# Two attention layers and two mixture-of-experts layers on one core: the small PSUM bank visited once per slot, the values product two slots behind, and one fp16 copy moved from ScalarE to VectorE

## What is computed

```python
xn = ln(x, g_norm)
q = (xn @ Wq).reshape(b, n, HEADS, DIM_HEAD).transpose(0, 2, 1, 3)
kv = xn @ Wkv
k, v = (kv[..., :DIM_HEAD], kv[..., DIM_HEAD:])
...
q = l2norm(q) * q_scale
k = l2norm(k) * k_scale
sim = jnp.einsum('bhid,bjd->bhij', q, k) * SCALE
...
sim = jnp.where(causal, neg, sim)
...
attn = jax.nn.softmax(sim, axis=-1)
out = jnp.einsum('bhij,bjd->bhid', attn, v)
out = out.transpose(0, 2, 1, 3).reshape(b, n, HEADS * DIM_HEAD)
return ln(out @ Wout, g_out)
```

## Time and profile before

| | |
|---|---|
| median of three runs | 1735.61 us |
| the profiled execution: its time | 1732.54 us |
| its span, first to last instruction | 1730.6 us |
| attention (first to last `probs`) | 90.0 to 1355.8 us |
| mixture of experts | from about 1370 us on |
| mean granted TensorE clock | 0.972 |

### The profile page before, as it was taken

One profiled execution on the slowest core, in us unless ns is written; L12 is line 12 of the kernel. 1 busy time (PEld: TensorE's weight loads), 2 busy tenths in 40 slices (PEclk: granted clock), 3 DMA queues, 4 the chain that ended last, 5 costly groups with the idle time before them and its releaser, 6 DMA issues.

```text
span 1730.6 us, 46424 instructions
## 1 busy us (share of the span) xinstructions
PE 1470.3 (85%) x16377; PEld 1081.0 (62%) x16377; DVE 1410.4 (81%) x3651; ACT 1210.2 (70%) x3064; POOL 751.0 (43%) x1412
## 2 busy tenths in 40 slices
PE   2467778888889999977888888999999799999998
PEld 1245556666677777766666666777777555555555
DVE  4557778888889999977788888999999687777777
ACT  1268778888889899978888888989999432332232
POOL 5557776443434334366554232223222365522222
PEclk9779999999999999989999999999999899999999
DMA  4002122111211223012121212221223000000000
GB/s 138 7 24 62 51 62 75 57 62 69 75 58 67 87 99 99 33 44 62 51 81 52 85 63 75 75 81 62 82 99 99 1 25 19 1 1 1 13 13 25
DMA packets 50440, 96.70 MB, mean 56 GB/s; under 512 B 3332, under 2 KB 27028, under 8 KB 50212
## 3 DMA queue, kind: packets, MB, share of 16 engines
q1 hardware_dynamic: 45504, 90.27, 15.8%
q10 hardware_dynamic: 4708, 3.45, 0.7%
HBM read 91.54 MB, written 2.17 MB: 54 GB/s over the span
## 4 chain that ended last, share of the span: by engine, by line
PE 42%; DVE 21%; ACT 14%; issue 11%; POOL 3%; DMA 1%; DVEq 0%; ACTq 0%; SPq 0%; POOLq 0%
PE tp L1312 7%; DVE p_lo L964 7%; ACT p_hi L722 6%; DVE biased L880 5%; PE sc L1203 3%; PE sc L1086 3%; PE sc L1087 3%; PE sc L1088 3%; ACT q_b L651 3%; PE sc L1204 3%; ACT probs L630 3%; PE op L1086 2%; PE aux L1086 2%; PE tp L1086 2%; PE aux L1088 2%
## 5 line engine op out<-in xcount | busy, mean ns | idle before, releaser
L964 DVE TENSOR_TENSOR p_lo<-tp,p_hi 128x512 f16<-128x512 f32 (+3 forms) x768 | 416.6, 554 | 121.3 <-ACT p_hi L722 114.3
L880 DVE CUSTOM_DVE_ANT_0 biased<-sc,bias,neg_null 128x256 f32<-128x256 f32 (+7 forms) x512 | 411.0, 803 | 2.7 <-issue 0.8
L630 ACT ACTIVATE probs<-biased,neg_max 128x256 f32<-128x256 f32 (+7 forms) x512 | 395.7, 773 | 14.2 <-DVE neg_max L880 12.7
L1312 PE MATMUL tp<-ident,probs 128*128 128x128 f32 x2304 | 388.7, 278 | 17.7 <-DVE p_lo L964 15.5
L722 ACT ACTIVATE p_hi<-tp 128x512 f16<-128x512 f32 (+3 forms) x768 | 368.9, 491 | 43.6 <-PE tp L1312 33.5
L1086 PE MATMUL op<-v_s,p_hi 128*128 128x64 f16 x2304 | 284.9, 194 | 54.4 <-DVE p_lo L964 35.9
L1203 PE MATMUL sc<-k_a,q_a 128*128 128x512 f16 (+3 forms) x768 | 254.2, 331 | 66.2 <-DVE neg_max L880 59.3
L1312 PEld LDWEIGHTS tp<-ident,probs 128*128 128x128 f32 x2304 | 267.9, 142 | 52.9 <-issue 37.9
L1088 PE MATMUL op<-v_s,p_lo 128*128 128x64 f16 x2304 | 284.0, 194 | 0.0
L1087 PE MATMUL op<-v_s,p_hi 128*128 128x64 f16 x2304 | 283.9, 194 | 0.0
L1086 PEld LDWEIGHTS op<-v_s,p_hi 128*128 128x128 f16 x2304 | 216.0, 99 | 85.5 <-DVE p_lo L964 62.1
(11 more groups left out here) (257 smaller groups left out, 3611.4 us busy)
## 6 DMA issues: line engine op xcount, KB each, us to landing
bias<-rel_table SPq DMA_DIRECT2D x4, 2048.0 KB, 8.5
bias<-in_fside_16xSxS SPq DMA_DIRECT2D x4, 2048.0 KB, 7.9
bias<-rel_table SPq DMA_DIRECT2D x4, 1792.0 KB, 7.9
bias<-in_fside_16xSxS SPq DMA_DIRECT2D x4, 1792.0 KB, 7.1
bias<-rel_table SPq DMA_DIRECT2D x4, 1536.0 KB, 7.3
bias<-in_fside_16xSxS SPq DMA_DIRECT2D x4, 1536.0 KB, 6.7
bias<-rel_table SPq DMA_DIRECT2D x4, 1280.0 KB, 5.6
bias<-in_fside_16xSxS SPq DMA_DIRECT2D x4, 1280.0 KB, 6.3
```

The lines of the kernel that those rows point to most:

```text
L630: ac.activation(probs[:, i % 2, 0:w], biased[:, i % 2, 0:w], ACT.Exp, bias=neg_max[:, u % 2, i % HU:i % HU + 1], scale=-1.0, accum_out=row ...
L880: ve.tensor_tensor_reduce(out=biased[:, i % 2, 0:w], in0=sc[i % 2][:, 0:w], in1=bias[:, g % 2, i % HU, 0:w], scale=-1.0, scalar=neg_null[: ...
L964: ve.tensor_tensor(p_lo[:, gi % 4, 0:nb * P], tp[gi % 2][:, 0:nb * P], p_hi[:, gi % 4, 0:nb * P], ALU.subtract).then_inc(s["p_lo"], 1)
L1312: last = te.transpose(tp[gi % 2][:, jj * P:(jj + 1) * P], probs[:, n % 2, (j0 + jj) * P:(j0 + jj + 1) * P], ident[:, :])
```

## The change

All of it lies in the per-slot order. TensorE: the small jobs come last in the slot, one per slot (k0 `null` and `y`, into different columns of one bank, k1 `q_proj`, k2 `q_t`, k3 `ot`), and the values product is that of slot n-2. Their evictions come at the start of the next slot: on ScalarE ahead of `probs`, on VectorE behind `biased`. `o_raw` and what hangs on it move one slot later, `q_t` one slot earlier. The copy `q_dup` is issued by VectorE, ahead of `q_lo`. The transposes of x move from n0-15 to n0-14. The numbers and sizes of all other instructions stay as they are.

```diff
-            return 0 <= n < N - 4 and all(plan.tile(i) < TILES // 2 for i in range(n + 1, n + 4))
+            return 0 <= n < N - 6 and all(plan.tile(i) < TILES // 2 for i in range(n + 1, n + 6))
...
                 first, second = banks(n)
+                was_first, was_second = banks(n - 1)
+                if k == 1 and 0 <= m - 2 < NU:
+                    u = m - 2
+                    act.wait_ge(s["y"], u + 1)
...
+                    ac.activation(dst, was_first[:, 0:D], ACT.Copy, scale=1.0 / WS).then_inc(s["y_s"], 1)
+                if k == 3 and 0 <= m + 2 < NU:
+                    u = m + 2
+                    act.wait_ge(s["q_t"], u + 1)
...
+                    for e in range(2):
+                        ac.activation(heads(q_b[0:DH, u % 2, :], e),
+                                      was_first[e * DH:(e + 1) * DH, 0:UW].rearrange("p (c q) -> p c q", q=P), ACT.Copy)\
+                            .then_inc(s["q_hi"], 1)
...
-                    act.wait_ge(s["q_hi"], 2 * (u + 1))
-                    ac.activation(q_a[0:DH, u % 2, :], q_b[0:DH, u % 2, :], ACT.Copy).then_inc(s["q_dup"], 1)
...
-                if k == 1 and 1 <= m <= NU:
+                was_first, was_second = banks(n - 1)
+                if k == 2 and 1 <= m <= NU:
                     u = m - 1
                     dve.wait_ge(s["o_null"], u + 1)
-                    dve.wait_ge(s["pv"], plan.groups_done(n - 2))
+                    dve.wait_ge(s["pv"], plan.groups_done(n - 3))
...
                     dve.wait_ge(s["q_hi"], 2 * (u + 1))
+                    ve.tensor_copy(q_a[0:DH, u % 2, :], q_b[0:DH, u % 2, :]).then_inc(s["q_dup"], 1)
...
+                if k == 1 and 0 <= m + 1 < NU:
...
+                    dve.wait_ge(s["q_null"], u + 1)
+                    if 0 <= m - 2 < NU:
+                        dve.wait_ge(s["y_s"], m - 1)
...
+                if k == 0 and 0 <= m - 2 < NU:
+                    u = m - 2
+                    dve.wait_ge(s["ot_hi"], u + 1)
...
+                now, before = plan.at(n), plan.at(n - 2)
...
+                if k == 0 and 0 <= m + 1 < NU:
+                    u = m + 1
+                    layer = u // U0
+                    pe.wait_ge(s["q_dup"], u + 1)
+                    pe.wait_ge(s["q_lo"], 2 * (u + 1))
...
-                if k == 3 and 0 <= m + 2 < NU:
+                if k == 2 and 0 <= m + 2 < NU:
...
-                now, before = plan.at(n), plan.at(n - 1)
...
+                if k == 3 and 0 <= m - 1 < NU:
+                    u = m - 1
+                    take(False, (s["ot_lo"], u + 1))
+                    pe.wait_ge(s["o_n"], u + 1)
```

More of the change, by code:

```diff
@@ L481, in _ @@
                         .then_inc(s["o_n"], 1)
-                if k == 2 and 0 <= m + 3 < U0:
+                if k == 3 and 0 <= m + 3 < U0:
                     u = m + 3
@@ L967, in _ @@
                         small()
-                if k == 1 and 0 <= m + 3 < U0:
+                if k == 2 and 0 <= m + 3 < U0:
                     u = m + 3
@@ new lines, in _ @@
+                now, before = plan.at(n), plan.at(n - 2)
+                for j in range(max(1, len(now), len(before))):
+                    if j < len(now):
+                        gi = now[j]
+                        _, j0, nb = plan.groups[gi]
+                        pe.wait_ge(s["probs"], n + 1)
+                        if gi >= 2:
+                            pe.wait_ge(s["p_lo"], gi - 1)
+                        for jj in range(nb):
+                            last = te.transpose(tp[gi % 2][:, jj * P:(jj + 1) * P],
+                                                probs[:, n % 2, (j0 + jj) * P:(j0 + jj + 1) * P], ident[:, :])
+                        last.then_inc(s["pt"], 1)
+                    if j < len(before):
+                        pv(before[j])
+                    if j == 0:
+                        small()
@@ new lines, in _ @@
+                if k == 0:
+                    after = []
+                    if 0 <= m - 2 < NU:
+                        after.append((s["y_s"], m - 1))
+                    if 0 <= m + 1 < NU:
+                        after.append((s["null"], m + 2))
+                    take(False, *after)
+                if k == 0 and 0 <= m + 1 < NU:
+                    u = m + 1
+                    layer = u // U0
+                    pe.wait_ge(s["q_dup"], u + 1)
+                    pe.wait_ge(s["q_lo"], 2 * (u + 1))
+                    if u == 0:
+                        pe.wait_ge(setup["big"], 1)
+                    for h in range(HU):
+                        cols = slice(h * P, (h + 1) * P)
+                        te.matmul(first[:, UW + h:UW + h + 1], q_a[:, u % 2, cols], kn_a[:, layer:layer + 1], start=True, stop=False)
+                        last = te.matmul(first[:, UW + h:UW + h + 1], q_b[:, u % 2, cols], kn_b[:, layer:layer + 1],
+                                         start=False, stop=True)
+                    last.then_inc(s["q_null"], 1)
@@ L1303, in _ @@
[L1303 to L1318 removed]
+                if k == 3 and 0 <= m - 1 < NU:
+                    u = m - 1
+                    take(False, (s["ot_lo"], u + 1))
+                    pe.wait_ge(s["o_n"], u + 1)
+                    o_f = o_n[:, :, :].rearrange("p h d -> p (h d)")
+                    for cc in range(UW // P):
+                        last = te.transpose(first[:, cc * P:(cc + 1) * P], o_f[:, cc * P:(cc + 1) * P], ident[:, :])
+                    last.then_inc(s["ot"], 1)
```

209 lines of the change are left out of this document (77 added, 132 removed).

## The result

The changed kernel takes **1900.09 us** (median of four runs, 1895.97 to 1902.61) against 1735.61 (four runs, 1735.16 to 1738.28); the ratio is 1.094, 95% interval 1.092 to 1.097. The forecast was 1770, range 1714 to 1796: slower it is, by 164.5 us and not by 34.

The account below looks back on a forecast made before the run. Short stages were taken as bound by hand-overs, long ones by TensorE and VectorE nearly full. Second layer 14, first 20, held-up copies 10, extra slot -10 gave +34 us on 1732.5, with 3.1 for the median 1770; range 1714 to 1796.

Parts of the forecast that it names:

- The bound: Short stages bound by hand-overs between engines, long ones by TensorE and VectorE nearly full; tile 7's unit 11.9 of 12.4 us.
- The copy: 64x512 fp16 `q_dup` on VectorE before `q_lo`: taken as 0.30 us each, 38 us for 128; leaves ScalarE, saving 80.6 there.
- The 10 us for copies held up by GpSimd: First layer: 64 VectorE copies exclude GpSimd's normalising of q, 0.15 us each, 10 us in all (bounds 0 and 26).
- The values product two slots behind: Removes at most 35.9 us of waits for `p_lo`; in heavy tiles `p_hi` waits for the product, slot loop 2.35 us.
- The link `q_t` to `ot`: `ot` needs the bank `q_lo` frees: 3.66 us against TensorE's 2.52 of work, so TensorE waits 1.1 us in tile 7.
- Tile 0's unit: Second layer, tile 0: the small jobs themselves form the chain, 6.15 us against 5.6, +0.6 us a unit.
- That the bank is not visited once per slot: Three of a tile's 32 slots: key, value and layer-norm jobs share `aux` with a small job in both versions; no effect.
- The extra slot between `xn` and its transposes, -10 us: Transposes of x one slot later after `xn`: saves about 0.6 us in each of 16 tiles, -10 us.
- The sum over "plain" units times eight: Second layer: each tile's change per plain unit (`q_n` to next `q_n`), summed over tiles and times 8 units, gives 14 us.
- The first layer's 0.1 us a unit more: First layer has two more instructions in the same stretch (`q_sq`, sum of squares), part hidden: 14 + 6 = 20 us.
- The rival "relief": ScalarE sets the pace; without the copy, half of `p_lo`'s 114.3 us wait for `p_hi` goes: 1717 us, chance 0.27.

Follow-up runs that it names:

- 1: Changed kernel with the copy of q's half back on ScalarE, behind `q_b`: 1893.9 us, ratio 1.091 to the kernel before.
- 2: Kernel before with only the copy moved to VectorE, ahead of `q_lo`: 1737.1 us, ratio 1.001 to the kernel before.
- 5: Changed kernel with the values product one slot behind again, rest of the new order kept: 1886.1 us, ratio 1.086 to the kernel before.
- 12: Changed kernel with useless transposes in light tiles (0 to 3), ten ahead of `ot` and four ahead of `y`: 1867.4 us, ratio 1.078 to the kernel before.
- 9: Changed kernel with VectorE's per-tile statistics and `xn` behind the slot's evictions, not ahead of them: 1889.1 us, ratio 1.089 to the kernel before.
- three edits together: Changed kernel with product one slot behind, statistics behind evictions, and six useless transposes before `ot` in light tiles: 1837.5 us, ratio 1.059 to the kernel before.

## Why the prediction was wrong

Its own steps, in order:

- *The bound* (short stages by hand-overs, long ones by two nearly full engines): right in kind. "TensorE can lose 0.5 us a unit there, no more" is the idle time that was left in a unit of 12.4 us, and no limit on how much longer the unit can get: the plain unit of tile 7 lost 0.9.
- *The copy*: 0.28 us for 0.30, right; no effect of its place to speak of (1, 2). The 10 us for copies held up by GpSimd did not come: in the first layer the 64 copies have a median of 0.28 us, as in the second, and only four take over 0.29 (the longest 0.61), less than 1 us in all.
- *The values product two slots behind*: right in kind, `p_hi` waits for it 62.1 us. It costs 14 us (5). The forecast let it gain in tile 4, 0.4 us a unit; the plain unit there gained 0.1 and the whole tile grew by 4.5 us.
- *The link `q_t` to `ot`*: right, and the largest wait of TensorE after. In tile 7 of the second layer it is 8.6 us in 7 units, 1.2 each where 1.1 was forecast. It was to be least in tile 4, and it is about the same there; in the light tiles, for which the forecast gave it no figure, it is 1.9 us a unit.
- *Tile 0's unit*: the chain was right link by link, and its sum of 6.15 us used TensorE's full speed. **This term was mis-sized**: with `y` and `q_proj` at the half clock, 1.0 us more, it comes near the 7.36 measured. The stretch of the earlier trace rows showed 0.87 for tile 0 before, and I read over it: a stage whose clock was already below 1, and which fell to 0.75 when waits were put into it. Refilling the waits gave 33 us back (12).
- *"That the bank is not visited once per slot"*, the point that the jobs of a tile still share `aux` ("that's in both versions and changes nothing"): **this step failed most plainly**, since it put at nothing a term that measures 29 us. Before, the projection stood at the slot's head and the per-tile job in its middle, with half a slot to the next user; now both stand in the later part and, in heavy tiles, the second waits for the first's eviction. Keys, and keys and values together, cost 15 and 29 us more in the new order than in the old.
- *The extra slot between `xn` and its transposes, -10 us*: **not borne out.** The fifth unit, which was to gain, grew by 32.4 us. The statistics ahead of `q_lo`, which the forecast did not count, are 11 of them (9), and the transposes of x now meet `q_t` in k2 (in the trace after, TensorE's `q_t` waits 11.3 us for `xt`'s eviction, 7 times). What the extra slot is worth by itself no run tells.
- *The sum over "plain" units times eight* was the frame that hid both: five units of eight are not plain. All 128 units were forecast at 34 us (14 and 20 for the two layers); the 48 plain ones alone took 26, the other 80 took 131.
- *The first layer's 0.1 us a unit more*: **mis-sized.** It lost 30 us more than the second, 0.5 us a unit; two thirds of that lie in its light tiles. No run looked for the cause.
- *The rival "relief"* falls with 2, and with `p_lo`'s wait for `p_hi`, which grew.

Runs put a price on 14 (product), 33 (clock in light tiles), 11 (statistics), 29 (two per-tile jobs) and 6 us (copy's place), 93 of 164.5 if they add, with 17 more where three of them are removed at once. Still open is how the rest, some 55 to 72 us, divides: the output's layer norm in the second and third unit (45.3 us by the trace; VectorE's 0.42 us and 0.41 us for it stand at the ends of k2 and k3, ahead of the slots with `q_lo` and `ot_lo`), the transposes of x in k2, the first layer's own work, and the clock in heavy tiles. None of these was tried alone.

No version of the new order beat the kernel before; the best, three edits together, is 5.9% slower than it.

## What to carry to other kernels

When jobs that share a buffer are moved, write down for each how long after the last eviction the next one is issued, and do it for the rare jobs too: an order that is clean in three units of eight can be lost in the other five. And where the granted clock of a stage is already below 1, put each new wait of TensorE down twice: once for itself, and once for the matmuls behind it at half speed if they are on the chain. And read the whole list of waits before, not the two that the change is meant to remove.

## What the hardware showed that I had not expected

Adding useless TensorE work made a kernel faster: 64 times six transposes gave 21 us and, with 64 times eight more, 33 us, while the granted clock rose from 0.931 to 0.949 and 0.969. The same trick in the kernel before raised the clock by 0.005 and gave nothing. A low clock is thus no price by itself; whether lifting it pays has to be tried in the kernel at hand.
